# All filler matmuls of TensorE given up in a six-stage decoder kernel

## What is computed

```
x = _layernorm(x + _L0_attn_ref(x, ...))        # linear attention, a scan over the tokens
x = _layernorm(x + _L0_xattn_ref(x, ctx, ...))  # cross attention, 16 heads, strided keys
x = _layernorm(x + _L0_ffn_ref(x, ...))         # hidden 512, a sine of the hidden values, relu
x = _layernorm(x + _L1_attn_ref(x, ...))        # state-space scan: 256 channels x 16 states
x = _layernorm(x + _L1_xattn_ref(ctx, x, ...))  # cross attention over context and latents
x = _layernorm(x + _L1_ffn_ref(x, ...))         # token shift, sigmoid and squared-relu gates
```

```
scores = einsum('bhqd,bhkd->bhqk', Q, Kg) * scaling; attn = softmax(scores)     # stage 2
q = hidden + quantum_phase * (w_imag * sin(theta + hidden * 0.1)) * 0.1         # stage 3
act = relu(q); out = act @ W2 + b2
h = h * exp(dt_t * A) + (dt_t * u_t) * B_t; y_t = h @ C_t + D * u_t             # stage 4
```

## Time and profile before

| | |
|---|---|
| median of 3 runs | 412.86 us (412.2 to 412.89) |
| the profiled execution | 410.33 us, its span 408.2 us |
| mean granted clock of TensorE | 0.954 |
| busy: PE, DVE, ACT, POOL | 83%, 78%, 52%, 55% of the span |
| L1449, the filler | 96 records, 23.9 us busy |

### The profile page before, as it was taken

One profiled execution on the slowest core, in us unless ns is written; L12 is line 12 of the kernel. 1 busy time (PEld: TensorE's weight loads), 2 busy tenths in 40 slices (PEclk: granted clock), 3 DMA queues, 4 the chain that ended last, 5 costly groups with the idle time before them and its releaser, 6 DMA issues. The chain is left out here.

```text
span 408.2 us, 5162 instructions
## 1 busy us (share of the span) xinstructions
PE 338.4 (83%) x1606; PEld 230.7 (57%) x1606; DVE 319.7 (78%) x642; ACT 211.6 (52%) x458; POOL 223.6 (55%) x226
## 2 busy tenths in 40 slices
PE   5538748789879669889888898898799999999991
PEld 2333447788666365423334453343388877898871
DVE  0599999998876953999999989989959544664537
ACT  2642222232252764998586424665546666664661
POOL 3499899992614003199799978998602700100012
PEclk9957959999989999999999999999999999999996
DMA  8900000000000000244344363444200000000001
GB/s 276 388 7 0 0 3 1 2 1 2 2 0 0 1 2 0 106 128 155 104 144 133 133 157 96 142 137 146 79 0 1 2 2 0 0 3 2 0 2 51
DMA packets 11521, 24.54 MB, mean 60 GB/s; under 512 B 1231, under 2 KB 2255, under 8 KB 11239
## 3 DMA queue, kind: packets, MB, share of 16 engines
q1 hardware_dynamic: 11495, 24.22, 18.2%
HBM read 23.63 MB, written 0.59 MB: 59 GB/s over the span
## 5 line engine op out<-in xcount | busy, mean ns | idle before, releaser
L1009 POOL TENSOR_TENSOR arena<-arena 128x512 f32<-128x512 f32 x63 | 79.5, 1276 | 23.6 <-DVE arena L643 23.1
L643 DVE TENSOR_TENSOR_SCAN arena<-arena,ps 128x512 f32<-128x512 f32 x64 | 77.2, 1207 | 0.0
L1645 PE MATMUL ps<-arena,first_in 128*128 128x512 f32 x128 | 66.3, 601 | 5.2 <-POOL arena L1009 4.7
L1252 ACT ACTIVATE arena<-arena,neg_a 128x508 f32<-128x508 f32 x64 | 43.4, 709 | 12.8 <-DVE arena L643 12.7
L1289 ACT ACTIVATE arena<-ps,arena 128x248 f32<-128x248 f32 x64 | 29.3, 462 | 38.9 <-DVE arena L674 38.9
L636 DVE TENSOR_TENSOR ps<-arena,ps 128x512 f32<-128x512 f32 x64 | 43.2, 677 | 4.0 <-PE ps L1633 3.5
L1054 POOL TENSOR_TENSOR rstd<-veps,mhalf 128x4 f32<-128x4 f32 (+2 forms) x6 | 5.2, 859 | 74.4 <-DVE veps L734 68.3
L1499 PE MATMUL ps<-arena,first_in 128*128 128x128 f32 (+1 forms) x256 | 31.8, 287 | 12.7 <-POOL arena L868 12.7
L1499 PEld LDWEIGHTS ps<-arena,first_in 128*128 128x128 f32 x256 | 30.8, 201 | 14.1 <-issue 8.1
L881 POOL TENSOR_TENSOR rstd<-veps,mhalf 128x4 f32<-128x4 f32 x8 | 8.2, 1022 | 55.4 <-DVE veps L392 41.1
L1645 PEld LDWEIGHTS ps<-arena,first_in 128*128 128x128 f32 x128 | 23.5, 192 | 19.9 <-POOL arena L1009 12.0
(11 more groups left out here) (281 smaller groups left out, 825.4 us busy)
## 6 DMA issues: line engine op xcount, KB each, us to landing
arena<-c_rows_dram SPq DMA_DIRECT2D x64, 256.0 KB, 3.2
fold_in<-in_fold_dram SPq DMA_DIRECT2D x1, 2056.0 KB, 13.9
late_in<-in_late_dram SPq DMA_DIRECT2D x1, 1422.5 KB, 17.3
early_in<-in_early_dram SPq DMA_DIRECT2D x1, 921.5 KB, 8.7
xres<-in_x_dram SPq DMA_DIRECT2D x1, 512.0 KB, 5.8
rows_in<-in_rows_dram SPq DMA_DIRECT2D x1, 512.0 KB, 14.8
kv_ctx<-in_context_dram SPq DMA_DIRECT2D x1, 480.0 KB, 10.1
first_in<-in_first_dram SPq DMA_DIRECT2D x1, 465.0 KB, 4.0
```

What stands on the lines that cost most here:

```text
L643: nc.vector.tensor_tensor_scan(hist[:, q % NBUF], fade[:, q % NFADE], chain(q), 0.0, ALU.mult, ALU.add).then_inc(S("scan"), 1)
L1009: tt(seen[:, q % NBUF], hist[:, q % NBUF], c_wide[:, q % NBUF], ALU.mult).then_inc(S("read_out"), 1)
L1252: act(fade[:, q % NFADE].rearrange("p (b t) -> p b t", t=T)[:, :, 1:], dt[:, n, cols(g)].rearrange("p (b t) -> p b t", t=T)[:, :, 1:], ACT ...
L1645: mm(y_bank, ident, seen[:, p % NBUF], start=False, stop=p % NS == NS - 1).then_inc(S("seen_used"), 1)
```

## The change

Every call of `stay_awake` and the helper are removed. Nothing else is changed: no matmul, wait, bank or order of any other work.

```
-            def stay_awake(n, k):
-                for _ in range(n):
-                    mm(bank(k)[:, 0:256], ident, W("xT")[:, 0:256], start=True, stop=True)
-
...
                 mm(bank(2, 2)[:, b * T:b * T + NK], s2_q[:, b * T:(b + 1) * T], key0[:, b],
                    start=True, stop=True).then_inc(S("score0"), 1)
-            stay_awake(6, 0)
...
                 mm(bank(2, 2)[:, b * D:(b + 1) * D], s2_oT[:, b * T:(b + 1) * T], W("wo0"),
                    start=True, stop=True).then_inc(S("projected"), 1)
-            stay_awake(8, 4)
...
             pe.wait_ge(S("gated"), 2)
-            stay_awake(6, 0)
             project3(0)
             project3(1)
-            stay_awake(6, 2)
...
             widen_b(1)
-            stay_awake(8, 0)
             pe.wait_ge(S("diag_d"), NH)
...
-                if 26 <= q < NK4 + 3:
-                    stay_awake(1, 4)
...
-                if NK4 + 5 <= q < NK4 + 10:
-                    stay_awake(1, 5)
```

## The result

The changed kernel takes 416.03 us (median of 4 runs, 415.25 to 418.26). The kernel before takes 412.88 us in the same comparison. The ratio is 1.012, with a 95% interval of 1.009 to 1.016: slower by 3.2 us, where 2.1 were forecast. The profiled execution took 418.26 us, the slowest of the four. It lies 7.9 us above the profiled execution of before (410.33), so the two traces show more than the medians do, and the difference has to be explained too.

What follows compares the result with a forecast made beforehand. VectorE was taken to bound the loop (busy 44.31 of 45.00 us). Terms 0.4 + 1.8 + 0.3 - 1.1 + 1.0 - 0.3 = +2.1 us gave 412.4 on the profiled scale, 415.0 on the median's; range 411.8 to 418.5.

Steps and rivals of the forecast that it cites:

- the four places that were named: Clock at 0.50 at stage 2's transposes and L1556, first hidden values, first half of stage 3's projection, first loop steps.
- the likeliest case: Whole kernel: a loss of 0.9 to 4.5 us, own range 413.7 to 417.4 us, chance 0.55.
- scores to probabilities: 6 fillers behind the scores: without them the clock falls before the second transposes, +0.4 us, highest +1.6.
- projection to hidden values: 8 fillers ahead of stage 3's hidden values: these begin at clock 0.50, +1.8 us (+1.0 to +3.0).
- projection of stage 3: 6 fillers ahead of it: cold first half loses 1.7 to 2.4 us, 1.5 us slack takes most, +0.3 (0 to +1.7).
- behind it: 6 fillers behind stage 3's projection hold up ready transposes: without them `narrow` starts earlier, -1.1 us (-2.4 to 0).
- ahead of the loop: 8 fillers in the wait for the first step sizes: loop begins at low clock, +1.0 us (0 to 2.0).
- inside the loop: 14 fillers, one ahead of a `widen_b` VectorE waits for: -0.3 us, lowest -0.4, highest +1.5 for a single fall.
- Every cold microsecond counts half: Rival: four new cold stretches, 14 to 27 us, cost half their time; about +8 us, 421 us, chance 0.08.
- The loop goes cold: Rival: at half clock TensorE falls behind VectorE's pace, 3 to 8 us over steps 26 to 41; about 420 us, chance 0.06.
- Faster: Rival: the clock is back before it counts, leaving only the gains -1.1 and -0.4; 411.3 us, chance 0.13.

Runs made afterwards that it cites:

- narrow fillers: The kernel before with all 48 filler matmuls, each of 8 columns instead of 256: 412.38 us against 412.28, ratio 1.002.
- the move: The kernel before with VectorE's L608 at step 13 and L650 at steps 25 and 54 ahead of their step's scan: 409.69 us against 412.10, ratio 0.995.

## Why the prediction was right, and where it was not

**The cause is right in kind, and its size is in part open.** The clock was low at the four places that were named, the fillers' instructions without their work give the same places, and VectorE is later behind each of them, in all three kernels without the work of the fillers. With the same VectorE order on both sides the fillers are worth 2.8 us by the medians. But the profiled executions put the price of the cold places ahead of the second L608 at 4.0, 1.5 and 1.7 us (the changed kernel, with narrow fillers, without fillers and with the move), and the kernel with the narrow fillers was not clearly slower than before. How much of the 3.2 us is the clock and how much is collisions that became more frequent isn't settled.

416.03 us lies in the likeliest case's own range, 1.0 us above the forecast. That it is so near is partly luck: in the profiled execution the terms came to 5.4 us instead of 2.1.

**The terms, by the lateness in the traces:**

| term | forecast | measured |
|---|---|---|
| scores to probabilities | +0.4 | +0.45; alone 0.0 |
| projection to hidden values | +1.8 (1.0 to 3.0) | +2.0 at the first angles; alone +2.2, in its trace +1.8 |
| projection of stage 3 | +0.3 (0 to 1.7) | +1.3 (3.79 - 2.47); alone -1.9, in its trace +0.7 |
| behind it | -1.1 | -1.0 (2.77 - 3.79); alone -1.2 |
| ahead of the loop | +1.0 (0 to 2.0) | +1.4 (below); alone +0.2, in its trace +1.1 |
| inside the loop | -0.3 (-0.4 to +1.5) | +1.2 (5.39 - 4.2); alone +1.4, in its trace -0.4 |
| sum | +2.1 | +5.4 in this trace |

For the loop's start: this L608 row of the changed kernel, against that of before, has its first start 2.8 us later (166.2 against 163.4) and its last 4.2 us later (198.9 against 194.7).

```profile
L608 DVE TENSOR_TENSOR arena<-arena x2: 679/1966/3254, 166.2 to 198.9; 32x512 f32<-32x512 f32 x2
```

*Projection of stage 3: the step that was too cheap.* The prediction let the first half lose 1.7 to 2.4 us and the slack of 1.5 us take most of it. L1570's first half was cold almost from start to end, because the clock had fallen at 142.4 and came back only at 152.7. It took 6.7 us instead of 3.84 and so lost 2.8, 1.3 more than the slack. VectorE waited 1.40 us for it, and its norm of the first half then held up the residual of the second: 157.94 directly behind the first half's, with no wait for TensorE. I had counted the slack of the first half alone, and not that both halves share one VectorE. Even 2.4 less 1.5 is 0.9 us, so +0.3 was low by its own numbers.

*Inside the loop: the wrong sign in this execution.* I took the quiet clock of 176 to 221 for the whole loop. But that stretch has other matmuls between the steps, and the fillers stand where there are none. At 241.4 the clock fell once, VectorE waited 2.20 us for a `widen_b`, and the step cost 1.2 us. The bound of +1.5 held. But this was one execution. The filler that stands ahead of a late `widen_b` is a real loss: in the traces without loop fillers, with narrow ones, and without any fillers and with the move, L636 at this place gained 0.4, 0.3 and 0.4 us, and a later fall, at 249.4 in the first two, cost nothing. For these three the forecast of -0.3 was right. The median of the run without loop fillers, +1.4, doesn't contradict it: its trace has its losses in stage 3 and at L650.

*Behind the projection: a sign that failed here.* The prediction wanted `narrow` 5.1 us behind the end of the projection instead of 6.2. It came 5.96 us behind it (162.86 against 156.90) instead of 6.07 (160.09 against 154.02 in the earlier trace rows), which is hardly nearer. The 1.0 us was won against the second half's norm, and in this execution that norm was held up by VectorE and not by the projection's end. So the term's size was right, and the distance was the wrong place to read it. Without fillers and with the move, where the second half waited for ACT, it was 5.34 us.

*The offset of 2.5 us between the profiled execution and the median.* I carried it over as a constant, and it isn't one. A single collision of L650 with GpSimd costs 2.5 us, one of the second L608 2.4, of which 0.5 is made up behind it, and an execution either has it or not. The profiled execution of before had it at L608 and not at L650; those of five of the six kernels with single groups left out had it at L650 (3.54 to 3.56 us). It also closes the sum: 5.4 us of clock and 2.5 of collision are the 7.9 between the two profiled executions. The medians differ by 3.2 only. That the timed executions of before mostly have the collision would account for it. The move that avoids it takes 2.4 us off the median, which speaks for this. So do the times of two single runs, which fall into two groups about 2.6 us apart: the one without the fillers ahead of the projection, given there, and the one without those behind it (five at 408.1 to 410.1 us, seven at 411.7 to 412.6). No trace of such an execution of before was taken, so it is argued and not shown.

**The rivals.** *Every cold microsecond counts half*: the stretches at half clock up to 244.8 are 6.9 + 6.8 + 10.3 + 6.9 + 3.4 = 34.3 us, 30.9 more than the 3.4 of the earlier trace rows, and half is 15.4 us. The trace has 5.4, since TensorE waits for others in much of the cold time. The Trainium skill's price ("TensorE: Matmul & The Clock Gate", section "Terms"), by which the 15.4 us are an estimate, came out about three times too high here. *The loop goes cold* came true behind its first steps for two stretches of 3.4 us only, of which one cost 1.2 us and the other nothing. *Faster* failed: the clock was low at the first L1563 and at the first loop steps. The singles don't add up to the whole (-0.1 + 2.2 - 1.9 - 1.2 + 0.2 + 1.4 = 0.6 us against 3.2): the intervals are 1 us each, and the one gain that its own trace doesn't show (-1.9) weighs most in it.

## What to carry to other kernels

Judge each filler matmul by its place: keep those ahead of dense work on which others wait, as at the hidden values (2.2 us), and take out any that stands in front of ready work, as behind the projection (1.2 us). A fall of the clock costs only what somebody waits for: two falls in the loop cost 1.2 us and nothing. Judge a clock loss where two halves share the engine behind, not by the slack of one half. When profiled executions and the median differ by a fixed step, look for an operation whose duration has two values before explaining anything else. Here moving it was worth 2.4 us, nearly as much as all fillers together, and the best kernel had the move, two groups of fillers less and three added fillers. Before reading a term out of one trace, look whether the same place comes out alike in other executions of the same code.

## What the runs showed of the hardware

- **A VectorE multiply that reads two SBUF operands can wait behind several GpSimd operations in a row.** Behind its scan L650 took 1.08 to 1.30 us or 3.54 to 3.56 us, and the second L608, with 32 rows, 0.84 to 0.85 us or 3.23 to 3.25. Ahead of the scan the long values were 2.22 to 2.23 and 2.55. Each long one ended 0.53 to 0.55 us behind the end of a GpSimd operation. L636, one of whose operands lies in PSUM, kept to 0.66 to 0.70 us in all its 64 steps beside the same GpSimd work. In the execution of before where L650 took 1.08 us, GpSimd's two L1009 took 2.94 us together instead of 2.49, so there GpSimd waited. The Trainium skill ("SBUF — State Buffer", section "Who interferes with whom") has the rule: an instruction with two SBUF inputs contends with a GpSimd instruction that reads SBUF. The trace agrees. What I hadn't expected is the length: the wait didn't end with the GpSimd operation that was under way, but went on over the next ones. Nor does the distance of the starts decide: the second L650 started 0.73 us behind the start of an L1009 in the execution of before (1.08 us long) and in that of the run without loop fillers (3.55 us long).
- **The clock falls at different places, or not at all, in executions of the same code.** The stretches at 0.50 between stage 2 and the loop's end were 3.4 us, 6.8 us or 10.3 us long. Up to the projection of stage 2 eight of the twelve kernels run the code of before. The clock fell at 116.9 to 118.7 us for 3.4 us in five of their profiled executions (before: 118.1). It didn't fall there in three: without the fillers ahead of the hidden values, without those in the loop, and with the move and without both groups at the projection of stage 3. Without that fall the value product took 2.01 us instead of 3.52, and VectorE's residual L379 came 1.5 us earlier in relation to the rows ahead of it. A forecast for one place can't be closer than that leaves open.
